# A second, features-first copy of the input for batches 2 to 7

## The reference

```
xn = layernorm(x)                                   # over features, no gain
for layer l = 0..3, for each direction d:
    z = sigmoid(h Wz + bz);  t = tanh(h Wh + bh)    # Wz = Wh = ctx[l], bz = bh = cond[l]
    s = linear_scan(1 - z, z t)                     # along the tokens, d sets the direction
    h = layernorm(s + h if l > 0 else s) * gamma + beta
x = x + concat(h_fwd, h_bwd) fusion_W' + fusion_b
x = x + proj(layernorm(gelu(layernorm(x) W_fc')))   # ternary weights
```

## Time and profile before

| | |
|---|---|
| median of three runs | 1540.54 us |
| the profiled execution | 1540.21 us, its span 1538.4 us |
| TensorE busy | 1518.7 us (99%) |
| VectorE busy | 1307.8 us (85%) |
| ScalarE busy | 1021.6 us (66%) |
| GpSimd busy | 829.6 us (54%) |
| granted TensorE clock | full throughout |

### The profile page before, as it was taken

One profiled execution on the slowest core, in us unless ns is written; L12 is line 12 of the kernel. 1 busy time (PEld: TensorE's weight loads), 2 busy tenths in 40 slices (PEclk: granted clock), 3 DMA queues, 4 the chain that ended last, 5 costly groups with the idle time before them and its releaser, 6 DMA issues.

```text
span 1538.4 us, 22933 instructions
## 1 busy us (share of the span) xinstructions
PE 1518.7 (99%) x7744; PEld 1202.7 (78%) x7744; DVE 1307.8 (85%) x2021; ACT 1021.6 (66%) x1688; POOL 829.6 (54%) x1013
## 2 busy tenths in 40 slices
PE   9999999999999999999999999999999999999999
PEld 7877888888888888888888877777777777777776
DVE  8998999999899989999888887786877777776786
ACT  7988789898687897787987444445454444444354
POOL 6766657578868678676788632331423333332331
PEclk9999999999999999999999999999999999999999
DMA  4211212321312112122044551030302020111000
GB/s 171 76 37 68 103 56 90 124 69 63 123 40 85 56 41 90 65 94 89 29 145 143 193 171 42 1 110 1 96 15 89 22 89 22 62 48 41 29 20 36
DMA packets 73157, 113.20 MB, mean 74 GB/s; under 512 B 5193, under 2 KB 37961, under 8 KB 69970
## 3 DMA queue, kind: packets, MB, share of 16 engines
q1 hardware_dynamic: 72754, 111.21, 21.3%
q10 hardware_dynamic: 288, 0.52, 0.1%
HBM read 73.95 MB, written 37.77 MB: 73 GB/s over the span
## 4 chain that ended last, share of the span: by engine, by line
PE 50%; DVE 2%; ACT 1%; issue 0%; POOL 0%; DVEq 0%; ACTq 0%; POOLq 0%
PE ps L639 15%; PE ps L620 14%; PE ps L572 11%; PE ps L499 6%; PE ps L519 1%; PE ps L585 1%; PE ps L533 1%; PE ps L649 1%; DVE bnp L1132 1%; PE ps L662 0%; ACT H L876 0%; DVE H L1120 0%; DVE yb L1112 0%; ACT AH L880 0%; DVE H L1121 0%
## 5 line engine op out<-in xcount | busy, mean ns | idle before, releaser
L499 PE MATMUL ps<-AH,WH 128*128 128x512 f32 x896 | 366.9, 409 | 7.8 <-DVE H L1121 6.1
L499 PE MATMUL ps<-AL,WH 128*128 128x512 f32 x896 | 351.0, 392 | 0.0
L499 PE MATMUL ps<-AH,WL 128*128 128x512 f32 x896 | 349.4, 390 | 0.0
L1587 POOL TENSOR_TENSOR H<-H,yb 128x512 f32<-128x512 f32 x192 | 245.9, 1291 | 8.5 <-DVE yb L1112 1.3
L1112 DVE TENSOR_TENSOR_SCAN yb<-ab,ps 128x512 f32<-128x512 f32 x192 | 231.9, 1208 | 15.5 <-POOL ab L1578 9.1
L950 ACT ACTIVATE g<-ps 128x512 f32<-128x512 f32 x128 | 76.5, 598 | 248.7 <-PE ps L620 248.7
L837 ACT ACTIVATE yb<-ps,ncnd 128x512 f32<-128x512 f32 x224 | 158.2, 706 | 87.3 <-PE ps L499 84.2
L499 PEld LDWEIGHTS ps<-AH,WH 128*128 128x128 f32 x896 | 168.5, 188 | 46.3 <-DVE H L1121 8.6
L1307 DVE SCALAR_TENSOR_TENSOR gl<-g,wbcol,gh 128x512 fp32r<-128x512 f32 x118 | 116.9, 991 | 97.7 <-ACT gh L960 97.6
L499 PEld LDWEIGHTS ps<-AL,WH 128*128 128x128 f32 x896 | 168.1, 188 | 37.1
L1688 POOL TENSOR_TENSOR rs<-mv,nhalf 128x1 f32<-128x1 f32 x32 | 43.0, 1342 | 282.2 <-DVE mv L1279 282.2
(11 more groups left out here) (193 smaller groups left out, 3230.4 us busy)
## 6 DMA issues: line engine op xcount, KB each, us to landing
hs_scratch<-H SPq DMA_DIRECT2D x16, 1024.0 KB, 5.4
hc<-hs_scratch SPq DMA_DIRECT2D x32, 512.0 KB, 4.4
xr<-in_x SPq DMA_DIRECT2D x32, 256.0 KB, 4.5
out<-ob SPq DMA_DIRECT2D x32, 256.0 KB, 2.2
xbuf<-in_x SPq DMA_DIRECT2D x7, 1024.0 KB, 7.6
RAW<-in_wt SPq DMA_DIRECT2D x16, 256.0 KB, 6.3
stg<-in_fct SPq DMA_DIRECT2D x16, 256.0 KB, 3.2
stg<-in_pjt SPq DMA_DIRECT2D x16, 256.0 KB, 2.9
```

The lines of the kernel that those rows point to most:

```text
L499: r = e.matmul(GATE[i % 3][:], w[:, q, m * 128:(m + 1) * 128], a[:, q, :], start=(n == 0), stop=(n == 11))
L1587: e.tensor_tensor(H[s][:, m, :], H[s][:, m, :], yb[i % 5][:], ALU.add).then_inc(s_v, 1)
```

## The change

For batches 2 to 7 the four transposing groups, `norm_x` and the per-piece `feature` and `low` of the input go. The host passes `x` a second time with features first (`xt`). Each batch is loaded twice into `xbuf`: once with tokens first for the mean and inverse deviation, and once features first. The two rows of 512 numbers are written to HBM (`put_moments`) and read back spread over all partitions (`load_turned`) into `xrow`. GpSimd subtracts one row and multiplies by the other (`center_x`, `scale_x`), in place, in four pieces of 128x512. ScalarE and VectorE then split halves of 128x1024 (`high_x`, `low_x`). The entries for `x` leave the tables of the `RING` and of the counts, and `mm` of such a job waits for `s_xl`.

```diff
@@ gpsimd
+        def center_x(b, q):
+            if q == 0:
+                e.wait_ge(d_xt, 16 * (b - 1))
+                e.wait_ge(d_rm, 32 * (b - 1))
+            e.tensor_tensor(xbuf[:, q, :], xbuf[:, q, :], xrow[:, 0, :], ALU.subtract).then_inc(s_xc, 1)
+        def scale_x(b, q):
+            e.wait_ge(s_xc, 4 * (b - 2) + q + 1)
+            e.tensor_tensor(xbuf[:, q, :], xbuf[:, q, :], xrow[:, 1, :], ALU.mult).then_inc(s_xk, 1)
...
             keep(job(s - 2), 0)
-            inv_x(batch(s + 1))
+            center_x(batch(s + 1), 1)
+            center_x(batch(s), 3)
+            inv_x(measured(s - 1))
             add(job(s - 3), 2)
+            scale_x(batch(s + 1), 1)
+            scale_x(batch(s), 3)
             add(job(s - 3), 3)
             keep(job(s - 2), 1)
             remains(s - 1)
             pieces(s - 1)
+            center_x(batch(s + 2), 0)
             add(job(s - 2), 0)
+            center_x(batch(s + 1), 2)
             inv(tail(s - 3), 0)
...
             keep(job(s - 2), 2)
+            scale_x(batch(s + 2), 0)
+            scale_x(batch(s + 1), 2)
@@ tensor, slot s
-            back("x", batch(s + 2), 2)
...
-            back("x", batch(s + 1), 0)
...
-            back("x", batch(s + 1), 1)
...
-            back("x", batch(s + 2), 3)
@@ scalar
+        def high_x(b, h):
+            s, p = 2 * (b % 2), slice(2 * h, 2 * h + 2)
+            e.wait_ge(s_xk, 4 * (b - 2) + 2 * h + 2)
...
+            e.activation(AH[s][:, p, :], xbuf[:, p, :], ACT.Copy).then_inc(s_xh, 1)
@@ vector
+        def low_x(b, h):
+            s, p = 2 * (b % 2), slice(2 * h, 2 * h + 2)
+            e.wait_ge(s_xh, 2 * (b - 2) + h + 1)
+            e.tensor_tensor(AL[s][:, p, :], xbuf[:, p, :], AH[s][:, p, :].bitcast(F32), ALU.subtract).then_inc(s_xl, 1)
...
-            input_stats(batch(s + 2))
+            input_stats(measured(s))
+            low_x(batch(s), 0)
@@ sync, at the end of slot s, after load_raw, put_by and store
+        def load_turned(b):
+            if b % 2 == 0:
+                e.wait_ge(s_xs, 4 * b + 8)
+            else:
+                e.wait_ge(s_xl, 2 * (b - 2))
+            e.dma_start(xbuf[:], xt_v[b]).then_inc(d_xt, 16)
+            e.wait_ge(d_xo, 32 * (b - 1))
...
+            for r in range(2):
+                e.dma_start(xrow[:, r, :], xrow_hbm[b, r].partition_broadcast(128)).then_inc(d_rm, 16)
...
+            if even(batch(s + 5)):
+                load_x(batch(s + 5) + 1)
+            if measured(s - 1) is not None:
+                put_moments(measured(s - 1))
+            if even(batch(s + 3)):
+                load_turned(batch(s + 3))
+            if even(batch(s - 1)):
+                load_turned(batch(s - 1) + 1)
```

More of the change, by code:

```diff
@@ L93, in batch, with even, measured @@
     return JOBS[job(s)][0] if job(s) is not None and JOBS[job(s)][2] == 0 else None
-LAST = len(TAILS) - 1
[L102 to L109, removed]
+def even(b):
+    return b is not None and b % 2 == 0
+def measured(s):
+    if even(batch(s + 5)):
+        return batch(s + 5)
+    return batch(s + 3) + 1 if even(batch(s + 3)) else None
+LAST = len(TAILS) - 1
+RING_SLOT = [("B", "b", 3, 2), ("B", "f", 2, 2), ("B", "f", 2, 0), ("B", "f", 2, 1), ("B", "b", 3, 3), ("B", "f", 2, 3),
+    ("B", "b", 3, 1), ("B", "b", 3, 0), ("T", "f", 1, 0), ("T", "b", 1, 0), ("T", "b", 2, 1), ("T", "f", 1, 1)]
+NORM_SLOT = [("b", 4, 0), ("f", 4, 1), ("f", 3, 0), ("b", 4, 1)]
+FEAT_SLOT = [("b", 5, 2), ("f", 4, 2), ("f", 4, 0), ("f", 4, 1), ("b", 5, 3), ("f", 4, 3), ("b", 5, 1), ("b", 5, 0)]
+LOW_SLOT = [("f", 4, 2), ("f", 4, 0), ("f", 4, 1), ("b", 5, 3), ("b", 5, 1), ("f", 4, 3), ("b", 5, 0), ("b", 4, 2)]
 STAT_SLOT = [("f", 3, 0), ("b", 3, 0), ("b", 4, 1), ("f", 3, 1)]
@@ L486, in mm @@
             for q in range(KC):
-                if m == 0:
+                if m == 0 and l == 0 and b >= 2:
+                    e.wait_ge(s_xl, 2 * (b - 2) + 1 + q // 2)
+                elif m == 0:
                     e.wait_ge(s_al, LOWS[("x", b, q) if l == 0 else ("h", TAIL[(b, d, l - 1)], q)])
@@ L877, in feature @@
                              scale=gam[:, m:m + 1]).then_inc(s_h, 1)
-            if what == "x" and idx >= 2:
-                e.wait_ge(s_mm, 4 * JOB[(idx - 2, 0, 3)] + 4)
             e.activation(AH[s][:, m, :], RING[n][:], ACT.Copy).then_inc(s_ah, 1)
+        def high_x(b, h):
+            if b is None:
+                return
+            s, p = 2 * (b % 2), slice(2 * h, 2 * h + 2)
+            e.wait_ge(s_xk, 4 * (b - 2) + 2 * h + 2)
+            if h == 0:
+                e.wait_ge(s_mm, 4 * JOB[(b - 2, 0, 3)] + 4)
+            e.activation(AH[s][:, p, :], xbuf[:, p, :], ACT.Copy).then_inc(s_xh, 1)
         def absolute(n):
@@ L1049, in _ @@
             gates(job(s - 2), 1)
-            feature("x", batch(s - 1), 0)
+            high_x(batch(s), 0)
             feature("h", tail(s - 4), 2)
@@ L1171, in input_stats @@
                     e.wait_ge(d_x1 if b == 1 else d_xb, 16 if b == 1 else 16 * (b - 1))
+                if i == 0 and b >= 4:
+                    e.wait_ge(d_xo, 32 * (b - 3))
                 e.bn_stats(bn[:, r, i, 0:6], (xbuf1 if b == 1 else xbuf)[:, i, :]).then_inc(s_xs, 1)
@@ L1465, in _ @@
             low("h", tail(s - 4), 2)
-            low("x", batch(s), 2)
-            low("x", batch(s - 1), 3)
+            low_x(batch(s - 1), 1)
             scan(job(s - 2), 1)
-            low("x", batch(s - 1), 0)
             low("h", tail(s - 4), 0)
@@ L1476, in _ @@
             stats(tail_b(s - 3), 0)
-            low("x", batch(s - 1), 1)
             low("h", tail_b(s - 5), 0)
@@ L1932, in _ @@
         for s in SLOTS:
-            if batch(s + 4) is not None and batch(s + 4) > 1:
-                load_x(batch(s + 4))
+            if even(batch(s + 7)):
+                load_x(batch(s + 7))
             if ABS0 <= s < ABS0 + 15:
```

46 lines of the change are left out of this document (37 added, 9 removed).

## The result

The changed kernel takes 1579.5 us (median of 4 runs, 1578.5 to 1580.7) against 1540.5: ratio 1.025, 95% interval 1.024 to 1.027. That is 39 us slower. The forecast was 18 us slower, and 1579.5 lies above the range, which ended at 1572.

The account below looks back on a forecast made before the run. TensorE was taken to set the pace in stage one, with GpSimd near its limit. On 1540.2 us, -3.5 + 11.5 + 5.1 + 1.8 + 3.3 = +18.2 gave 1558 us; range 1543 to 1572.

Parts of the forecast that it names:

- Direction: Whole kernel: slower was given 0.82, same 0.06, faster 0.12.
- That is everything the change can gain: TensorE in batches 2 to 7: 24 transposing groups of 0.43 us go, saving 10.4 us, 1.73 a batch.
- is not waited for: ScalarE: it loses more work than it gains, and nobody waits for it; no time was priced.
- Next to no change: VectorE: 24 low operations of 0.67 us go, 12 low_x of 1.18 come, 14 us for 16.
- port: Rival: low_x and GpSimd hinder each other where GpSimd is saturated, 9 to 13 us more, 1567 to 1571; chance 0.15.
- GpSimd's term: GpSimd's added work less idle time, saving included: batch 6 +5.1, batch 4 +11.5, 5 and 7 +1.8, 2 and 3 -3.5.
- Batches 2 and 3: GpSimd's 12.6 us of idle time hold 10.1 of work, so the saving stays: -3.5 us, bounds -3.5 and +3.
- Batch 4's load: GpSimd waits 6.5 us for the turned load behind load_raw(9), 5.1 more than for batch 6; batch 4 +11.5 us.
- Batch 2's: SP's load for batch 2, held behind the weights' first reading, might come late; covered by the bound of +3.
- Batch 6's: GpSimd, ready at about 582.1, waits 1.4 us for batch 6's turned load and rows, there at 583.5.
- Moments: VectorE's moments moved into slots 22 and 36 delay a low and a back group: 1.65 us twice, +3.3.

Follow-up runs that it names:

- b2: a1 with high_x and low_x cut to two columns a partition, so layer 0 multiplies stale data: 1537.6 us, ratio 0.998.
- a4: The kernel before with only the moments, inv_x and load of even batches 2, 4 and 6 moved three slots ahead: 1543.6 us, +3.1.
- c2: a1 with low_x alone cut to two columns, high_x left whole: 1537.7 us, ratio 0.998.
- a1: The changed kernel without GpSimd's 48 centring and scaling operations, input left uncentred and unscaled in batches 2 to 7: 1549.0 us, ratio 1.0055.
- c3: The changed kernel with each low_x replaced by two bn_stats of 512 columns, low part left out: 1574.5 us, 5.0 less than the changed kernel.
- a2: The kernel before plus 48 scratch GpSimd operations of 128x512 at the places of center_x and scale_x: 1568.7 us, +28.3.
- a3: The changed kernel with SP's turned load of an even batch put ahead of load_raw, reaching batches 4 and 6: 1574.5 us, -5.0.
- c4: The changed kernel with GpSimd's operations placed as in b3, moments one slot earlier, turned load ahead of load_raw, everything computed: 1569.7 us.
- b3: a2 with its 48 operations placed singly ahead of keep and inv, over four slots instead of three: 1548.2 us, +7.6 on the kernel before.
- b1: a1 with low_x replaced by two tensor_scalar operations of the same shape with one SBUF operand each: 1558.0 us.
- c1: a1 with each low_x replaced by two bn_stats of 512 columns over the same input, low part left out: 1541.4 us, ratio 1.0007.
- d1: c4 with each low_x replaced by two bn_stats with one SBUF operand, low part left out: 1557.7 us, ratio 1.011.

## Why the forecast was wrong

- **Direction**: right. TensorE's saving cannot pay for what comes.
- **"That is everything the change can gain", 10.4 us**: as a bound right, as a term of the sum wrong. 6.2 us come (b2, with a4's 3.1 added back). I took each group as time of TensorE alone and wrote that ScalarE "is not waited for". TensorE's waits for ScalarE's tokens went from 1.8 to 4.6 us with no other new work in the way (c2), and to 9.0 in the changed kernel. At least 1.1 of those 2.8 us follow a weight load behind batch 4's moved load, which I had not priced either.
- **"Next to no change" for VectorE** is the step that failed most. I compared 14 us of `low_x` with 16 of `low` and priced the difference. `low_x` measured 1.38 us in the median and up to 2.09, since it shares with GpSimd what the old `low`, with one operand in PSUM, did not. In a1 its length is 3.7 us and its meetings 7.6, where I had 0; in the whole kernel the meetings are 5.0 (c3). The rival *port* was thus right in kind, on top of the forecast and not in its place, and too high in size: 9 to 13 us, where c3 gives 5.0. Its 1.1 to 1.6 us are what one meeting adds to the two operations (0.9 on GpSimd and 0.4 on VectorE at 631 us), but most of that does not reach TensorE. I took stage two's median as evidence against it, from a stretch where GpSimd seldom works.
- These two and the moments make a1: -6.2 + 3.7 + 7.6 + 3.1 = +8.2 (measured 8.6; the terms are differences of the same runs, so that the sum is bound to come near), where I had -10.4 + 3.3 = -7.1. Of the 21 us missed, 15.7 are here.
- **GpSimd's term**: 14.9 + 10.4 of saving in it = 25.3 forecast, 30.5 measured (changed less a1). The size is near, the accounting wrong. I subtracted a window's waits from its added work. In a queue that runs in order, idle time counts only if it stands between the new operation and the next `add` that TensorE wants. Batches 2 and 3 were to be free and cost 8.3 us (a2). The neighbouring terms hid this, since a nearly full window gives the same answer by both accounts.
- **Batch 4's load**: the wait is right, 6.4 us for 6.5, and its piece near, 14.3 for 13.2. Its price is not: I took all 5.1 us that it is longer than batch 6's as time, and without it the piece is 5.0 shorter only because 2.0 of half clock go too (a3). **Batch 2's**, bounded by +3, waited 3.6 us at 159.92. **Batch 6's** 1.4 us did not come: GpSimd was late itself.
- **Moments**: right in size, 3.1 for 3.3, with some luck: the two places that I priced give 2.8, and a third gives 0.6.
- **The clock**: not considered at all. Some 3 us in the changed kernel, and 10 in c4.

## What to carry to other kernels

Price an added operation of an in-order queue by what stands behind it up to the next result that a busier engine wants, slot by slot, less the spare time there; a window's sum of idle time tells nothing about that, and moving the same 48 operations was worth 20 us (a2 against b3). In the whole kernel the same move, with two others, gave 10 (c4), since other engines' waits took its place. When an operand moves from PSUM to SBUF, the operation's length in a quiet stretch is not its price: look where GpSimd runs beside it. Look also at what stands behind a load that is moved forward in a queue. And a removed operation of the busiest engine need not be worth its length, here 6.2 of 10.4 us.

## What was not expected of the hardware

The meetings look like a lock, not like shared bandwidth: in a1 at 631 us, whichever of `low_x` and GpSimd's operation comes second stands still until the first ends, to within 0.13 us, and then takes its full time. In the changed kernel:

```profile
L1171 DVE TENSOR_TENSOR AL<-xbuf,AH x12: 1200/1381/2091, 197.2 to 735.1; 128x1024 fp32r<-128x1024 f32 x12
L1605 POOL TENSOR_SCALAR ab<-yb x224: 612/614/1633, 16.9 to 907.3; 128x512 f32<-128x512 f32 x112
```

The columns are minimum, median and maximum in ns: a 0.61 us clamp took 1.63 beside a `low_x`. The page "SBUF — State Buffer" of the Trainium skill, section "SBUF: two separate sides", says just this: an exclusive lock, held for the whole instruction, taken by a VectorE operation with two SBUF inputs (against a GpSimd operation that reads SBUF) or in a two-port mode. The traces agree, with 2.15 for 1.29 us above. By b1 a `tensor_scalar` with one SBUF operand is caught too, and by c1 `bn_stats` is not.

TensorE's clock fell to half behind a wait of 6.7 us and behind several of 1.8 to 2.0, but not behind every one of that length: in the changed kernel it fell after 1.88 us at 678.5 and did not after 1.90 at 457.6, in d1 it did not after 1.93, and in a2 not after 2.13 at 250.1. Behind the waits of 1.5 to 1.7 us for VectorE in c1 it never did. What decides between them stays open. The cost is in the rows: 0.43 instead of 0.23 us for each of up to eight matmuls.
